# A table stage buffer stored and refilled in two parts instead of one

## The reference, cut to what matters

```python
k = typed_linear(x, Wk, ntype, 3).reshape(n, H, D)     # 3 node types
q = typed_linear(x, Wq, ntype, 3).reshape(n, H, D)
v = typed_linear(x, Wv, ntype, 3).reshape(n, H, D)
k_e, v_e, q_e = k[src], v[src], q[dst]
for r in range(5):                                     # 5 edge types (relations)
    m = (etype == r)[:, None, None]
    kw = kw + jnp.where(m, jnp.einsum('ehd,hdf->ehf', k_e, Ratt[r]), 0.0)
    mv = mv + jnp.where(m, jnp.einsum('ehd,hdf->ehf', v_e, Rmsg[r]), 0.0)
a = (kw * q_e).sum(-1) * pri[etype] / sqrt(D)
...                                                    # softmax over each dst, weighted sum, Wa, skip, layernorm
...                                                    # second layer: 16 relation weights, gates, segment sum, relu, layernorm
```

## Time and profile before

| | us |
|---|---|
| median of 3 runs | 2108.01 (2104.2 to 2119.34) |
| the profiled execution, its own time | 2111.33 |
| span of the profiled execution | 2109.7 |
| table phase in that span | 0 to 343.2 |
| layer 1's edge phase | 343.2 to about 1440 |
| layer 2's edge phase | about 1440 to the end |

### The profile page before, as it was taken

The page is one execution under the profiler, slowest core; times in us unless marked ns, Lnnn a source line. Parts: engine busy times, 40 slices in busy tenths (PEclk is TensorE's granted clock), DMA queues, the critical chain, the costliest instruction groups (busy, mean ns, idle before and its releaser), DMA issues.

```text
span 2109.7 us, 21535 instructions
## 1 busy us (share of the span) xinstructions
PE 1386.6 (66%) x6758; PEld 1135.8 (54%) x6758; DVE 926.7 (44%) x1940; ACT 494.7 (23%) x1069; POOL 854.6 (41%) x905
## 2 busy tenths in 40 slices
PE   4899985785797667777677776679425444445444
PEld 3888884574675556665466655567313322233323
DVE  5533454764564455454465544654212322223321
ACT  2223322232333333233243332335100000000000
POOL 1130004754244332233432334320575666666662
PEclk8999996798798878889888887789656666656666
DMA  5444465655445544445544455443433333333331
GB/s 122 124 147 144 135 227 157 183 181 174 136 142 176 161 146 137 133 134 160 178 145 142 149 157 176 141 136 95 115 109 89 104 104 104 104 94 107 108 104 53
DMA packets 103847, 286.54 MB, mean 136 GB/s; under 512 B 20804, under 2 KB 40408, under 8 KB 100660
## 3 DMA queue, kind: packets, MB, share of 16 engines
q0 software_dynamic: 56032, 169.34, 26.6%
q1 hardware_dynamic: 47774, 116.71, 18.3%
HBM read 189.33 MB, written 96.65 MB: 136 GB/s over the span
## 4 chain that ended last, share of the span: by engine, by line
PE 46%; issue 23%; another core or an unknown queue 12%; DVE 8%; DMA 5%; ACT 2%; POOL 2%; SPq 1%; DVEq 0%; ACTq 0%; POOLq 0%
PE bank L953 12%; PE bank L863 9%; PE bank L835 8%; PE bank L727 4%; PE bank L793 4%; DMA kv_table<-tstage 4%; PE bank L781 3%; DVE kv L1371 2%; PE bank L749 1%; POOL kv L649 1%; PE bank L735 1%; DVE onehot_r L1363 1%; PE bank L755 1%; DVE S L1376 1%
## 5 line engine op out<-in xcount | busy, mean ns | idle before, releaser
L633 POOL DMA_INDIRECT kv<-kv_table,idx x416 | 424.1, 1019 | 637.9 <-DVE idx L1358 514.7
L649 POOL DMA_INDIRECT kv<-message_table,rows x416 | 394.4, 948 | 274.1 <-issue 123.4
L953 PE MATMUL bank<-kv,onehot_w 128*121 128x256 f32 x832 | 274.7, 463 | 338.0 <-issue 307.2
L953 PEld LDWEIGHTS bank<-kv,onehot_w 128*121 128x121 f32 x832 | 186.2, 226 | 426.5 <-issue 391.0
L835 PE MATMUL bank<-wr_r,x1T_r 128*121 128x512 f32 x1248 | 359.5, 433 | 34.9 <-issue 22.7
L835 PEld LDWEIGHTS bank<-wr_r,x1T_r 128*121 128x121 f32 x1248 | 235.7, 200 | 95.2 <-issue 28.5
L1097 ACT ACTIVATE mstage<-bank,gate 121x256 f32<-121x256 f32 x416 | 171.4, 471 | 245.3 <-PE bank L835 132.7
L863 PE MATMUL bank<-kv,onehot_r 128*121 128x264 f32 x832 | 204.0, 394 | 0.0
L1512 DVE SCALAR_TENSOR_TENSOR z<-bank,xb 121x256 f32<-121x256 f32 x26 | 10.9, 420 | 425.5 <-remote 280.8
L863 PEld LDWEIGHTS bank<-kv,onehot_r 128*121 128x121 f32 x832 | 151.3, 187 | 29.5
L854 PE MATMUL bank<-ident,carry 8*128 8x8 f32 x26 | 6.2, 237 | 241.9 <-DVE carry L1441 220.3
(11 more groups left out here) (136 smaller groups left out, 1647.1 us busy)
## 6 DMA issues: line engine op xcount, KB each, us to landing
message_table<-mstage SPq DMA_DIRECT2D x104, 484.0 KB
kv_table<-tstage SPq DMA_DIRECT2D x26, 1210.0 KB
kv<-kv_table,idx POOLq DMA_INDIRECT x416
kv<-message_table,rows POOLq DMA_INDIRECT x416
query_table<-qstage_r SPq DMA_DIRECT2D x26, 242.0 KB
qb_r<-query_table SPq DMA_DIRECT2D x26, 242.0 KB
kv<-in_Wr POOLq DMA_DIRECT2D x2, 2048.0 KB, 14.8
xb<-in_x SPq DMA_DIRECT2D x26, 121.0 KB
```

What stands on the lines that cost most here:

```text
L633: pool.indirect_dma_start(kv[:, par, u, 0:2 * C], None, ktab, bass.IndirectOffsetOnAxis(ap=idx[:, par, u:u + 1], axis=0)).then_inc(kv_land ...
L649: pool.indirect_dma_start(mrows[:, r.q, u, :], None, mtab, bass.IndirectOffsetOnAxis(ap=rows[:, 1, r.number, u:u + 1], axis=0)).then_inc(l ...
L953: last = mm(b_l[r.q][:NODES, 0:C], onehot_w[:, r.q, u, :], mrows[:, r.q, u, :], start=(u == 0), stop=(u == U - 1))
```

## The change

A tile's table is stored by two DMAs: relations 0 to 2 (121 rows of 6144 bytes) once the jobs q = 0 to 3 are evacuated, and relations 3 and 4 (121 rows of 4096 bytes) once q = 4 and 5 are too. The semaphore of each stage buffer becomes two, one for each part, and a copy into a buffer waits only for its own part (`q // 4`). `last_of_part` picks the last evacuation that part 0 needs (jobs with q < 4), or, for part 1, the last of the tile. VectorE's final wait covers four semaphores. To make room for the two new semaphores, `grid_ready` and `fill_ready` are merged into `count_step`, waited for at 1, 2 and 3 in the same places.

```diff
@@ -305,12 +305,12 @@
             "const_ready", "zeroed", "rel_ready", "ident_high"))
         pool_step = sem("pool_step")
         counted = sem("counted")
-        alpha_exp, grid_ready, meta_step = sem("alpha_exp"), sem("grid_ready"), sem("meta_step")
+        alpha_exp, count_step, meta_step = sem("alpha_exp"), sem("count_step"), sem("meta_step")
         cnt_summed, starts_ready, tables_over, mask_ready = (sem(n) for n in (
             "cnt_summed", "starts_ready", "tables_over", "mask_ready"))
         xm_ready, x_filled, x_high, x_low, t_filled, t_act, t_dve = (sem(n) for n in (
             "xm_ready", "x_filled", "x_high", "x_low", "t_filled", "t_act", "t_dve"))
-        t_stored, q_stored = sems("t_stored", 2), sems("q_stored", 2)
+        t_stored, q_stored = [sems(f"t_stored{k}_", 2) for k in range(2)], sems("q_stored", 2)
 
         q_loaded, x_loaded = sems("q_loaded", 2), sems("x_loaded", 2)
         idx_ready, oh_ready = sems("idx_ready", 2), sem("oh_ready")
@@ -342,7 +342,7 @@
             "l_z", "l_st", "l_mv", "l_sd", "l_rstd", "l_y"))
         l_out = sem("l_out")
 
-        fill_ready, overfull_ready = sem("fill_ready"), sem("overfull_ready")
+        overfull_ready = sem("overfull_ready")
         g_in, g_idx, g_rows, g_landed, g_scored, g_stored, g_out, g_less, g_exp, g_weighted, g_summed, g_next, g_link = (
             sem("g_" + n) for n in ("in", "idx", "rows", "landed", "scored", "stored", "out", "less", "exp",
                                     "weighted", "summed", "next", "link"))
@@ -379,9 +379,9 @@
             def on_dve(self, k):
                 return self.jobs[k][0] != "tab" or not self.on_act(k)
 
-            def last_of_tile(self, nth, t):
-
-                return max(n for k, n in nth.items() if self.jobs[k][:2] == ("tab", t))
+            def last_of_part(self, nth, t, part):
+
+                return max(n for k, n in nth.items() if self.jobs[k][:2] == ("tab", t) and (self.jobs[k][2] < 4 or part))
 
             def query(self, nth, t):
 
@@ -419,7 +419,7 @@
 
             _, t, q = job
             st = tstage[:NODES, t % 2, :, :]
-            eng.wait_ge(t_stored[t % 2], s * 32 + 16 * (t // 2))
+            eng.wait_ge(t_stored[t % 2][q // 4], s * 32 + 16 * (t // 2))
             if q < 4:
                 return st[:, 0:3, q * P:(q + 1) * P], b[:NODES, 0:3 * P].rearrange("p (r n) -> p r n", r=3)
             kk = q - 4
@@ -430,7 +430,8 @@
         @block.sync
         def _(sp):
             for k in range(2):
-                sp.sem_inc(t_stored[k], 32)
+                for part in range(2):
+                    sp.sem_inc(t_stored[k][part], 32)
                 sp.sem_inc(q_stored[k], 32)
             sp.dma_start(nt_i[:NODES, :], nt_rows).then_inc(ld_types, 16)
             x_tiles = x.rearrange("(j p) c -> p j c", p=NODES)
@@ -450,9 +451,11 @@
             sp.dma_start(x_all[:, SUPER:TILES, :], x_tiles[:, SUPER:, :]).then_inc(ld_x, 16)
 
             def store_table(s, plan, t, to):
-                sp.wait_ge(t_act, s * NA + plan.last_of_tile(plan.nth_on_act, t))
-                sp.wait_ge(t_dve, s * ND + plan.last_of_tile(plan.nth_on_dve, t))
-                sp.dma_start(to, tstage[:, t % 2, :, :].rearrange("p r c -> p (r c)")).then_inc(t_stored[t % 2], 16)
+                for part, (a, b) in enumerate(((0, 3), (3, ET))):
+                    sp.wait_ge(t_act, s * NA + plan.last_of_part(plan.nth_on_act, t, part))
+                    sp.wait_ge(t_dve, s * ND + plan.last_of_part(plan.nth_on_dve, t, part))
+                    sp.dma_start(to[:, a * 2 * C:b * 2 * C], tstage[:, t % 2, a:b, :].rearrange("p r c -> p (r c)")
+                                 ).then_inc(t_stored[t % 2][part], 16)
 
             def store_queries(s, plan, t, to):
                 sp.wait_ge(t_act, s * NA + plan.query(plan.nth_on_act, t))
@@ -1274,8 +1277,8 @@
             low_part(rel_r[:, 1, :, :, :, :], rel[:, :, :, :, :], rel_r[:, 0, :, :, :, :]).then_inc(rel_low, 1)
             mix()
             dve.wait_ge(ld_grid, 16)
-            v.tensor_copy(grid_f[:, :], grid_i[:, :]).then_inc(grid_ready, 1)
-            dve.wait_ge(grid_ready, 1)
+            v.tensor_copy(grid_f[:, :], grid_i[:, :]).then_inc(count_step, 1)
+            dve.wait_ge(count_step, 1)
             count(range(EARLY))
             dve.wait_ge(ld_x, 16)
 
@@ -1310,10 +1313,10 @@
 
             dve.wait_ge(starts_ready, 1)
             v.tensor_scalar(fill[:, ROUNDS - 1:], starts[:, ROUNDS - 1:], -1.0, float(E), ALU.mult, ALU.add)
-            v.tensor_tensor(fill[:, 0:ROUNDS - 1], starts[:, 1:], starts[:, 0:ROUNDS - 1], ALU.subtract).then_inc(fill_ready, 1)
-            dve.wait_ge(fill_ready, 1)
-            v.tensor_reduce(most[:, :], fill[:, :], AX.X, ALU.max).then_inc(fill_ready, 1)
-            dve.wait_ge(fill_ready, 2)
+            v.tensor_tensor(fill[:, 0:ROUNDS - 1], starts[:, 1:], starts[:, 0:ROUNDS - 1], ALU.subtract).then_inc(count_step, 1)
+            dve.wait_ge(count_step, 2)
+            v.tensor_reduce(most[:, :], fill[:, :], AX.X, ALU.max).then_inc(count_step, 1)
+            dve.wait_ge(count_step, 3)
             v.tensor_scalar(overfull[:, :], most[:, :], -float(ROUND_EDGES), 0.0, ALU.add, ALU.max).then_inc(overfull_ready, 1)
             with dve.Fori(2, META) as s:
                 table_step(s)
@@ -1348,7 +1351,8 @@
             table_step(STEPS, final)
 
             for k in range(2):
-                dve.wait_ge(t_stored[k], 16 * (ROUNDS // 2 + 2))
+                for part in range(2):
+                    dve.wait_ge(t_stored[k][part], 16 * (ROUNDS // 2 + 2))
             dve.wait_ge(x_low, STEPS * NX)
             dve.wait_ge(ident_high, 1)
             v.memset(den[:, :], 1.0).then_inc(tables_over, 1)
```

## The result

The changed kernel takes **2084.77 us** (median of 4 runs, 2082.49 to 2088.98) against 2107.84 (4 runs, 2104.2 to 2119.34) of the kernel before: a ratio of 0.9888, 95% interval 0.9856 to 0.992, 23 us less. The forecast was 2098, range 2090 to 2110. The profiled execution took 2082.82, with a span of 2081.2; of before it was 2111.33 and 2109.7, so the pair of traces differs by 28.5 us, 5.4 more than the medians.

The account below looks back on a forecast made before the run. TensorE was taken to bound the table phase, held up by waits for table stores. Stalls -8.0, end -0.7, clock -1.0 and edits +0.1 sum to -9.6 us: 2098 us for the median, range 2090 to 2110.

Parts of the forecast that it names:

- The stalls (-8.0): Table phase, six steps: tile 3's copies no longer wait for tile 1's store, gaining 7.3 to 9.1 us, taken as 8.0.
- The rate of the shorter rows: Table stores: rows of 6144 and 4096 bytes move at 0.95 of the whole rows' rate, bounds no cost and 0.71.
- The end of the phase (-0.7): Last two table stores: issued 1.55 us earlier, the phase ends 0.7 us earlier, range -1.55 to +1.2.
- The clock (-1.0): Two wide kvT blocks behind stalls: with shorter gaps both keep TensorE's full clock (-3.1 us) or neither; taken as -1.0 us.
- Of which I have assumed that they only shift: The two phases behind the table phase: they begin earlier and are otherwise unchanged.
- Repeats and the later phases add 4 us on each side: Whole kernel: repeats and later phases, whose clock wanders, widen the range by 4 us on each side.
- the repeats' spread of 15 us: Whole kernel: repeats spread by some 15 us, so about 1% (21 us) can be told from no change.
- 1: Rival, table phase: part of the stall stays, by a rate 10 to 20% lower or another wait; -3 us, 2105; chance 0.14.
- 2: Rival, store queue: each store pays its own landing, up to 2.0 us, so the stall stays; 2110 us; chance 0.06.
- 3: Rival, store queue becomes the bound below rate factor 0.82; at 0.71 it is +27 us, 2135; chance 0.04.
- The 2.0 us for a DMA: Table stores: a fixed cost of about 2.0 us per DMA, which paid in sequence would give the time of rival 2.
- Rival 4: Table phase: clock losses go, tail gains 1.55, stalls 9.1; -13.7 us, 2094; chance 0.75 together with the forecast.

Follow-up runs that it names:

- g_split_only: Changed kernel with both parts issued only at the tile's end and the refill waiting for both, short rows kept: 2158.73 us, 0.9954 of the kernel before.
- e1: Changed kernel, but a copy into a stage buffer waits for both parts of its last store: 1701.6 us, 0.9919 of the kernel before.
- e2: Changed kernel, but both parts are issued only when all six jobs of a tile are evacuated: 1702.78 us, 0.9928 of the kernel before.
- l_two_whole: Kernel before, each table stored by two DMAs of 66 and 55 whole 10240 byte rows: 2174.23 us, 1.0021 of the kernel before.
- e4_third: Kernel before, whole stores, with a third stage buffer for tile 3 in steps 2 to 5: 1708.38 us, 0.9964 of the kernel before.
- the second pair: Kernel before and changed kernel, both unaltered, run again on another chip: 2170.22 and 2154.54 us, the latter 0.9924 of the kernel before.
- the last job: Last chip's runs: kernel before (2116.61 us), it and the changed kernel delayed by 13 additions, changed kernel (0.9909), and that with 112 and 9 row stores (0.9891).
- The three later comparisons: Changed kernel, unaltered, run again against the kernel before in three jobs on other chips: ratios 0.9924, 0.9943 and 0.9909.
- the first pair: Profiled executions of the kernel before and the changed kernel in the first result: 2111.33 and 2082.82 us; table phase 15.1 us shorter.
- f_before: Kernel before, unaltered, run again for its profile on another chip: 2170.22 us, ratio 1.0.

## Why the prediction was wrong

Two kinds of terms failed: the small ones of the table phase (the clock and the tail, and the sign of the rows' rate), which took its gain from 9.6 to 15.1 us, and the allowance for everything behind the phase, which then left the median outside the range.

- **The stalls (-8.0): right in size.** 8.2 us measured, no tstage copy waits, the step is 43.46 us (43.6 forecast), the gap 0.54 us (under 1.2). As the text said, TensorE's own end is then what is late.
- **The rate of the shorter rows: the wrong side.** "I take 0.95", and the bounds reached only down, from 1 to 0.71. It is above 1: 16.8 us on average against 19.2 for the same bytes issued alike. In the changed kernel's step 4 tile 1's last part landed 17.0 us after the first issue, where the forecast had 19.3 to 20.3. I read the message stores' equal busy time per byte as "no cost" and had no case in which shorter rows gain. Had I been more open there, g_split_only would have been a rival: the short rows alone nearly remove the stalls. So most of the stalls' gain came from a term that the forecast had as a cost. That the earlier issue and the refill by parts would have sufficed at an unchanged rate, as the prediction's sums say, no run shows.
- **The end of the phase (-0.7): mis-sized.** 2.2 us. The first store left 1.55 us earlier, as forecast, and e1 against e2 puts the earlier issue at 1.7 to 2.0; what is left for the rows is 0.2 to 0.6, and l_two_whole has as much with whole rows (15.1 against 15.4).
- **The clock (-1.0): mis-sized, the term that failed most in the phase.** It gave 4.7. Its bound was -3.1 from two wide blocks; the last, narrow block, 10.02 us instead of 8.39, wasn't looked at, although the prediction says that the table phase is TensorE's. And the choice of a third of the bound was a guess between "both" and "neither": in the twelve profiles without the stall, 72 blocks after the first, none lost its clock; in the five of kernels that keep it throughout (e4_third aside) one to four of six did. How much that is depends on the execution of the kernel before: 1.6 us in the second pair, where -1.0 would have been near.
- **"Of which I have assumed that they only shift": the allowance of 4 us for repeats and later phases took the forecast out of its range.** In the phase it was 15.1 us against 9.6; from 2108 that is 2093, inside the range. The other 8 us of the median's 23 lie in phases that the change doesn't touch. Moving their start by 9 us shifted the end by about that much, so the assumption holds of the mean; but the edge phase of the changed kernel differs by 30 us between two executions on chips of nearly the same time, and medians of four runs on each side don't average that out. "Repeats and the later phases add 4 us on each side" was too little, and the repeats' spread of 15 us, read off three runs, was over 30 us in the 29 runs of the last job. The range allowed for up to 18 us less than 2108. The three later comparisons (13.2, 9.8 and 17.4 us) lie inside that, and the first, 23.1, doesn't: that much of the miss is luck.
- **Rivals.** 1, 2 and 3 are refuted: no wait stayed, more stores cost nothing that shows, and the queue didn't become the bound. The 2.0 us for a DMA that the prediction took from the Trainium skill (DMA: Bandwidth & Descriptors, section "Anatomy of one DMA") are given there for DMAs that GpSimd issues; these are SyncE's, and no run here shows them paid one after the other. Rival 4, "it does what it says and more", is the nearest to the first pair (-13.7 against 15.1); the forecast's -9.6 is the nearer one to the other two (10.7 and 11.4). Its terms are not quite what happened either: stalls 8.2 and not 9.1, clock 4.7 and not 3.1.

## What to carry to other kernels

Where an engine stands still behind a late landing, count its slower block afterwards as part of the stall, the last block too: here the clock added a fifth to more than half of the waiting itself again. Before a store is called slow or fast, try its rows: cut to a middle length (of three tried here, only 6144 and 4096 bytes gained), and with a number of rows that all 16 DMA engines can share; neither needs a new wait. And take the spread of a phase that the change doesn't touch from several executions before giving a range; one trace can't show it.

## What wasn't expected of the hardware

**One program, 1715 and 2168 us.** The table phase, without its stalls, is the same on all chips to about a microsecond (end at 328.65, 327.41, 327.87, 327.56); layer 1's edge phase is not. On the slow ones VectorE's add of z stands for up to 16 us. The waits, before's from 200 to 1500 us, then e1's, on the chip of 1715 us:

```profile
DVE z L1401 <- remote: 261.3, 21, 16.2
```

```profile
DVE z L1406 <- PE bank L815: 45.9, 25, 8.4
```

In the timeline of the changed kernel's first profile it starts just when a run of GpSimd's gathers is over, and GpSimd's next gather waits for the idx copy that VectorE makes later:

```profile
762.31 0.95 POOL L636 DMA_INDIRECT kv<-kv_table,idx  x1 [0.30 <-issue]
764.69 0.42 DVE L1405 TENSOR_TENSOR z<-z,bank 121x256 f32<-121x256 f32 x1 [14.71 <-remote]
788.36 0.95 POOL L636 DMA_INDIRECT kv<-kv_table,idx  x1 [25.10 <-DVE idx L1362]
```

In e1 the same add comes in the midst of the gathers:

```profile
774.63 0.95 POOL L637 DMA_INDIRECT kv<-kv_table,idx  x1 [0.30 <-issue]
775.18 0.42 DVE L1406 TENSOR_TENSOR z<-z,bank 121x256 f32<-121x256 f32 x1 [1.61 <-PE bank L815]
775.88 0.95 POOL L637 DMA_INDIRECT kv<-kv_table,idx  x1 [0.30 <-issue]
```

So on some chips the two engines take turns, at 42 to 48 us a round instead of 30, and TensorE's granted clock in that phase is 0.84, where e1's is 0.98 with a DMA share of 0.67 (columns as in rows 2):

```profile
343.20:1157.00 813.80, 755.56 (x4136) 633.31 (x4136) 611.28 (x1066) 378.87 (x853) 464.46 (x409) 0.98 0.67 211
```

What holds the add wasn't tried. The edge phase of f_before took 1197.2 us and that of e1 828.7: 370 us, more than twenty times the change of this study.
